# GNN kernel: whole-row unpack, sums, catch-up and epilogue at other places, 64-column pairs, DVE scaling of the last groups

## The reference

```python
# layer 0
deg = jnp.clip(jnp.sum(adj, axis=1, keepdims=True) + 1.0, 1.0, None)
h_neigh = (adj @ X + X) / deg
z = jnp.concatenate([X, h_neigh], axis=1) @ W + b
out = jax.nn.relu(z); norm = jnp.linalg.norm(out, axis=1, keepdims=True)
layer0 = out / jnp.maximum(norm, 1e-12)
x = _layernorm(x + layer0)
# layer 1
deg = jnp.sum(adj, axis=1, keepdims=True)
neigh = adj @ x / (deg + 1.0)
x = _layernorm(x + jnp.concatenate([x, neigh], axis=-1) @ W1.T)
```

## Time and profile before

| | |
|---|---|
| median of 3 runs | 778.35 us (778.16 to 779.37) |
| profiled execution | 778.61 us |
| its span, first to last instruction | 776.7 us |
| granted TensorE clock, mean | 0.96 |
| PE busy | 662.5 us, 85% |
| PEld busy | 610.1 us, 79% |
| DVE busy | 710.8 us, 92% |
| ACT busy | 619.5 us, 80% |
| POOL busy | 211.1 us, 27% |
| read from HBM | 270.6 MB |

### The profile page before, as it was taken

One profiled execution on the slowest core, in us unless ns is written; L12 is line 12 of the kernel. 1 busy time (PEld: TensorE's weight loads), 2 busy tenths in 40 slices (PEclk: granted clock), 3 DMA queues, 4 the chain that ended last, 5 costly groups with the idle time before them and its releaser, 6 DMA issues.

```text
span 776.7 us, 28012 instructions
## 1 busy us (share of the span) xinstructions
PE 662.5 (85%) x11173; PEld 610.1 (79%) x11173; DVE 710.8 (92%) x2703; ACT 619.5 (80%) x848; POOL 211.1 (27%) x302
## 2 busy tenths in 40 slices
PE   1457777878788888989899999999999999999992
PEld 0357677878677787878798989989998989988992
DVE  4699988999999999999999999999999999988894
ACT  4879798999989898989898988887888988840037
POOL 2225433535333332424313030211102020201024
PEclk9978897989999999999999999999999999999997
DMA  9999999999999999999999999999999999800004
GB/s 302 386 420 420 416 410 420 420 419 419 417 420 421 402 420 404 418 416 415 413 402 418 381 420 372 400 360 408 381 398 386 395 383 387 349 2 3 3 21 93
DMA packets 46125, 274.55 MB, mean 353 GB/s; under 512 B 12647, under 2 KB 12711, under 8 KB 13223
## 3 DMA queue, kind: packets, MB, share of 16 engines
q1 hardware_dynamic: 45184, 270.55, 87.0%
q0 software_dynamic: 576, 2.10, 0.8%
q10 hardware_dynamic: 230, 0.07, 0.0%
HBM read 270.60 MB, written 2.10 MB: 351 GB/s over the span
## 4 chain that ended last, share of the span: by engine, by line
DVE 31%; PE 27%; DMA 12%; issue 12%; ACT 10%; POOL 7%; ACTq 0%; DVEq 0%; SPq 0%; POOLq 0%
PE s_ps L367 13%; DMA a_in<-in_adj 9%; DVE e L766 9%; ACT junk L557 7%; DVE t_sb L773 6%; POOL small L1119 6%; PE u_ps L385 4%; PE p_ps L353 3%; DMA xl<-in_x 3%; DVE q_sb L839 2%; DVE y_sb L833 2%; DVE u_sb L773 2%; DVE a_in L773 1%; PE z_ps L431 1%; PE p_ps L442 1%
## 5 line engine op out<-in xcount | busy, mean ns | idle before, releaser
L557 ACT ACTIVATE junk<-a_in 128x2048 uint8<-128x2048 uint16 x256 | 489.6, 1919 | 3.1 <-DMA a_in<-in_adj 3.0
L367 PE MATMUL s_ps<-xh,t_sb 128*128 128x129 f16 x4096 | 377.9, 247 | 22.9 <-DVE t_sb L773 20.2
L367 PEld LDWEIGHTS s_ps<-xh,t_sb 128*128 128x128 fp8e4 x4096 | 306.2, 100 | 50.5 <-DVE t_sb L773 24.7
L766 DVE TENSOR_SCALAR e<-a_in 128x2048 fp8e4<-128x2048 f32 x256 | 310.7, 1224 | 7.8 <-DMA a_in<-in_adj 6.9
L1127 POOL COPY store<-pk 128x32 uint32<-128x32 uint32 (+1 forms) x250 | 130.2, 562 | 312.0 <-ACT pk L566 312.0
L353 PE MATMUL p_ps<-pow_bf,e 128*128 128x16 bf16 x4096 | 141.8, 170 | 62.7 <-DVE e L766 58.9
L353 PEld LDWEIGHTS p_ps<-pow_bf,e 128*128 128x128 fp8e4 x4096 | 128.9, 96 | 79.2 <-DVE e L766 72.9
L773 DVE TENSOR_SCALAR t_sb<-pk 128x128 uint32<-128x128 uint32 x1024 | 150.8, 222 | 5.3 <-ACT pk L566 4.8
L1119 POOL TENSOR_TENSOR small<-small,minus_half 128x4 f32<-128x4 f32 x32 | 74.6, 2332 | 203.9 <-DVE small L827 162.5
L385 PE MATMUL u_ps<-xh,u_sb 128*128 128x128 f16 x1488 | 99.2, 218 | 0.0
L385 PEld LDWEIGHTS u_ps<-xh,u_sb 128*128 128x128 fp8e4 x1488 | 88.9, 97 | 1.2
(11 more groups left out here) (110 smaller groups left out, 486.9 us busy)
## 6 DMA issues: line engine op xcount, KB each, us to landing
a_in<-in_adj SPq DMA_DIRECT2D x256, 1024.0 KB, 10.3
xl<-in_x POOLq DMA_DIRECT2D x4, 512.0 KB, 16.1
out_h<-e SPq DMA_DIRECT2D x8, 256.0 KB, 2.6
b_sb<-in_L_gnn_b ACTq DMA_DIRECT2D x3, 0.2 KB
w_sb<-in_L_gnn_W ACTq DMA_DIRECT2D x1, 32.0 KB
w_raw<-in_L_gnn_W ACTq DMA_DIRECT2D x1, 32.0 KB
```

The costliest lines, as they stand in the source:

```text
L367: last = nc.tensor.matmul(s_ps[:, n % 2, at:GW], t_sb[:, b, :], xh[:, b, at:GW], start=(b == 0), stop=False)
L557: nc.scalar.activation(junk[:, t % 2, :], halves[t % R], ACT.Copy, scale=1.0 / 128, accum_out=half_sum[:, n, c:c + 1]).then_inc(s_half, 1)
L766: nc.vector.tensor_scalar(e8[:, c, :], a_in[:, t % R, :], 1.0, None, ALU.is_equal, saturate=False).then_inc(s_e, 1)
```

## The change

- **Unpack**: a whole row at once (8 operations instead of 16 half as wide), and t_sb has two buffers. s_t and s_sum count whole rows.
- **Order on PE**: in block n the quarters are now 1, 2, 3 of block n-2 and 0 of block n-1; the catch-up of block n-1 is in chunks 0 and 1 of block n. transpose_cat is behind the quarter of (k, c) = (2, 2), dense ahead of pack (2, 3), transpose_h at the end of (3, 3), dense_h behind pack (0, 1) of the next block. Weights are taken after block 0's packs.
- **Order on DVE, ScalarE and POOL**: moved to match. low_part and begin_acc now stand between compare (n,1) and compare (n,2) of a block with k = 0.
- **Pairs**: catch-up and the tail sums of the second half use two accumulated matmuls of 64 columns with the same weights, in place of one of 128; DVE then adds once instead of twice.
- **End**: the last group's squares and their sums are made by DVE, and DVE scales output groups 4 to 7 with one operation each.
- **Buffers**: h_sb, h_t, w1_raw and the small bias tiles now lie in other tiles.

```diff
+NA = 4
-        t_sb = sb("t_sb", [P, NB, P], FP8)
+        t_sb = sb("t_sb", [P, 2, NB, P], FP8)
+        h_t = cat_t[0:F, :, :]
+        w1_raw = agg_flat[0:F, 0:P]
+        def quarter(n, c):
+            return (n - 1, 0) if c == 3 else (n - 2, c + 1)
@@ sync
-                sp.wait_ge(s_o, g + 1)
+                if g < NA:
+                    sp.wait_ge(s_o, g + 1)
+                else:
+                    sp.wait_ge(s_o_dve, g - NA + 1)
@@ tensor
             def sum_quarter(n, i):
-                if i % 2 == 0:
-                    pe.wait_ge(s_t, n * 2 + i // 2 + 1)
+                if i == 0:
+                    pe.wait_ge(s_t, n + 1)
...
             def catch_up(n, half_of):
...
                     for b in range(W):
-                        last = nc.tensor.matmul(u_rows[:, r, :], u_sb[:, r * W + b, :],
-                                                xh[:, low(q - 1) + b, 0:HP], start=(b == 0), stop=(b == W - 1))
+                        for part in range(2):
+                            last = nc.tensor.matmul(u_rows[:, r, 0:F], u_sb[:, r * W + b, :],
+                                                    xh[:, low(q - 1) + b, part * F:(part + 1) * F],
+                                                    start=(b + part == 0), stop=(b + part == W))
...
-            for n in range(NB):
+            for n in range(1, NB):
                 e, k = n // BR - 1, n % BR
-                if e >= 0 and k == 2:
-                    dense(e)
                 for c in range(NC):
+                    if e >= 0 and (k, c) == (2, 3):
+                        dense(e)
                     pack_chunk(n, c)
-                    if e >= 0 and (k, c) == (1, 3):
+                    if e >= 1 and (k, c) == (0, 1):
+                        dense_h(e - 1)
+                    if n > 1 or c == 3:
+                        sum_quarter(*quarter(n, c))
+                    if n > START[1] and c < 2:
+                        catch_up(n - 1, c)
+                    if e >= 0 and (k, c) == (2, 2):
                         transpose_cat(e)
-                    if n == START[seg(n)] and n and c == 0:
-                        pe.wait_ge(s_glo, low(seg(n)) // BR)
-                    if n:
-                        sum_quarter(n - 1, c)
-                    if e >= 0 and (k, c) == (3, 0):
+                    if e >= 0 and (k, c) == (3, 3):
                         transpose_h(e)
-                    if n >= START[1] and c in (1, 2):
-                        catch_up(n, c - 1)
-                    if e >= 0 and (k, c) == (3, 1):
-                        dense_h(e)
             e = NE - 1
+            sum_quarter(NB - 2, 1)
+            dense_h(e - 1)
+            catch_up(NB - 1, 0)
+            sum_quarter(NB - 2, 2)
+            catch_up(NB - 1, 1)
+            sum_quarter(NB - 2, 3)
@@ scalar
                 sum_codes(n, 0)
-                if e >= 0 and k == 2:
-                    take_z(e)
+                if e >= 1 and k == 0:
+                    take_h(e - 1)
+                if n:
+                    take_packed(n - 1, 1)
                 sum_codes(n, 1)
-                if n:
-                    take_packed(n - 1, 1)
-                if n >= 2:
-                    take_sums(n - 2)
-                if e >= 0 and k == 3:
-                    take_h(e)
+                if e >= 1 and k == 0:
+                    take_g(e - 1)
                 sum_codes(n, 2)
                 take_packed(n, 0)
-                if e >= 0 and k == 3:
-                    take_g(e)
+                if e >= 0 and k == 2:
+                    take_cat(e)
                 sum_codes(n, 3)
-                if e >= 0 and k == 1:
-                    take_cat(e)
+                if n >= 2:
+                    take_sums(n - 2)
+                if e >= 0 and k == 2:
+                    take_z(e)
...
-            for g in range(NV + 1):
-                if g < NV:
-                    squares(g)
-                if g:
+            for g in range(NV - 1):
+                squares(g)
+                if 1 <= g <= NA:
                     finish(g - 1)
@@ vector
-            def unpack(n, h):
-                dve.wait_ge(s_pk, n * 2 + h + 1)
-                if n:
-                    dve.wait_ge(s_sum, (n - 1) * 2 + h + 1)
+            def unpack(n):
+                dve.wait_ge(s_pk, n * 2 + 2)
+                if n >= 2:
+                    dve.wait_ge(s_sum, n - 1)
...
-                link(nc.vector.tensor_tensor(rows, u_rows[:, 0:r1 - r0, 0:F], rows, ALU.add))
-                nc.vector.tensor_tensor(rows, u_rows[:, 0:r1 - r0, F:HP], rows, ALU.add).then_inc(s_uadd, 1)
+                nc.vector.tensor_tensor(rows, u_rows[:, 0:r1 - r0, 0:F], rows, ALU.add).then_inc(s_uadd, 1)
...
+            def last_variance():
+                rows = slice(NB - TG, NB)
+                dve.wait_ge(s_vadd, 2 * NV)
+                dve.wait_ge(s_fvar, NV - 4)
+                for n in range(NB - TG, NB):
+                    ins = nc.vector.scalar_tensor_tensor(out=sqf[:, (NV - 1) % 4, n % TG, :], in0=acc[:, n, :], scalar=1.0,
+                                                         in1=acc[:, n, :], op0=ALU.mult, op1=ALU.mult,
+                                                         accum_out=fvar[:, 1, n:n + 1])
+                link(ins)
+                nc.vector.scalar_tensor_tensor(out=fvar[:, 1, rows], in0=fvar[:, 1, rows], scalar=1.0 / F,
+                                               in1=fvar[:, 0, rows], op0=ALU.mult, op1=ALU.add).then_inc(s_fvar, 1)
+            def scale_rows(g):
+                rows = slice(g * TG, (g + 1) * TG)
+                dve.wait_ge(s_froot, g + 1)
+                dve.wait_ge(s_out[g % 4], 16)
+                nc.vector.tensor_tensor(o_sb[:, g % 4, :, :], acc[:, rows, :], bc(fvar[:, 1, rows], TG),
+                                        ALU.mult).then_inc(s_o_dve, 1)
...
                 compare(n, 0)
-                if n:
-                    unpack(n - 1, 0)
                 if e >= 0 and k == 3:
-                    normalise(e)
-                if n > START[1]:
-                    add_piece(n - 1)
+                    norm(e)
                 compare(n, 1)
-                if n >= START[1]:
-                    unpack_piece(n)
                 if e >= 0 and k == 2:
-                    norm(e)
+                    mean(e)
+                if e >= 1 and k == 0:
+                    low_part(e - 1)
+                    begin_acc(e - 1)
                 compare(n, 2)
                 if n:
-                    unpack(n - 1, 1)
-                if e >= 0 and k == 1:
-                    mean(e)
+                    unpack(n - 1)
+                if e >= 0 and k == 3:
+                    residual(e)
                 compare(n, 3)
+                if n > START[1]:
+                    add_piece(n - 1)
+                if n >= START[1]:
+                    unpack_piece(n)
+                if e >= 0 and k == 3:
+                    normalise(e)
...
-                if e >= 0 and k == 2:
-                    residual(e)
-                if e >= 0 and k == 3:
-                    low_part(e)
-                    begin_acc(e)
...
             for g in range(NV):
+                if g >= 4:
+                    variance(g - 1)
+                if g >= NA + 2:
+                    scale_rows(g - 2)
                 add_tail(NV + g)
...
-            variance(NV - 1)
+            last_variance()
+            scale_rows(NV - 2)
+            scale_rows(NV - 1)
```

More of the change, by code:

```diff
@@ L161, in gnn_kernel @@
         b0_sb = sb("b0_sb", [3, F], F32)
[L162 to L165, removed]
         b0_rows = sb("b0_rows", [3, BR, F], BF16)
         ones_bf = sb("ones_bf", [3, P], BF16)
+        h_t = cat_t[0:F, :, :]
+        b0_rest, b0_sum, b0_one = (q_sb[0:3, i, :] for i in range(3))
+        b0_part = q_sb[0:3, 3, 0:F // 2].bitcast(BF16)
         x_in = xl[:, :, 0:F]
@@ L364, in sum_quarter @@
                     pe.wait_ge(s_xlo, i + 1)
+                if n + 1 < NB and n + 1 == START[seg(n + 1)] and n and i * CB < lows(n):
+                    pe.wait_ge(s_glo, min(lows(n), (i + 1) * CB) // BR)
                 for b in range(i * CB, (i + 1) * CB):
                     at = 0 if b < lows(n) else HP
-                    last = nc.tensor.matmul(s_ps[:, n % 2, at:GW], t_sb[:, b, :], xh[:, b, at:GW],
+                    last = nc.tensor.matmul(s_ps[:, n % 2, at:GW], t_sb[:, n % 2, b, :], xh[:, b, at:GW],
                                             start=(b == 0), stop=False)
@@ L441, in tail_sums @@
                     for b in range(W):
-                        last = nc.tensor.matmul(v_ps[j % 3][:, r, :], v_sb[:, j % VR, r * W + b, :],
-                                                xh[:, at + b, 0:HP], start=(b == 0), stop=(b == W - 1))
+                        if j < NV:
+                            last = nc.tensor.matmul(v_ps[j % 3][:, r, :], v_sb[:, j % VR, r * W + b, :],
```

(22 more changed lines are left out.)

79 lines of the change are left out of this document (41 added, 38 removed).

## The result

The changed kernel takes 813.61 us (median of 4 runs, 812.86 to 815.08) against 778.62 (4 runs, 778.16 to 779.37): a ratio of 1.0451, 95% interval 1.0433 to 1.0469. Forecast were 796.0 and a range of 775 to 806. The direction was right and the size was not: +35 us in place of +17.8. The profiled execution has a span of 811.1 (before: 776.7).

A forecast was written before the change was run, and what follows sets the result against it. The adj transfer bounds the first half, then PE, full from block 44, with DVE fuller just before. The last sum ends at 722.0, 24.0 later; less 6.2 at the end gives +17.8 on 778.35: 796 us, range 775 to 806.

The forecast's parts named there:

- Whole-row unpack, "can give back 2.9": Blocks 28-35: cheaper DVE unpack and one add fewer bring block 36 forward by 2.9 us, ends 0 and 5.8.
- the lock: At low_part DVE waits for PE's dense_h, PE for compares queued behind; priced at 19.7 us from block 36.
- The new place of low_part, 19.7 us: Behind dense_h, DVE's delayed compares make PE wait three times a group; 19.7 us in seven groups, 0 to 24.
- dense right behind transpose_cat, 0.83 each: PE waits 0.83 us for ScalarE's copy, seven times from block 36 on: 5.8 us.
- the rival in which only the middle wait remains: Behind dense_h PE still has queued work, so 7 x 1.37 us replaces 19.7: 786 us, chance 0.11.
- the 3.0 behind transpose_h: PE's wait of 0.43 us behind transpose_h is kept, seven times from block 36 on: 3.0 us.
- Work moved past the stream, 5.8: Later sums, catch-up and one dense_h add 5.8 us of PE work from block 36 on, with nothing to cover it.
- Pairs, 0 (-3.9 to 3.9): Catch-up and tail: 1544 pairs of 64-column matmuls at 55.9 ns, as one of 128 columns; no change, ends -3.9 and +3.9.
- The end, -6.2: Behind PE's last tail sum 9.2 us remain instead of 15.4: 6.2 us saved, between 5 and 7.5.
- Start, 0: Block 0 no longer waits for weights, but later blocks go at the transfer's rate: 0, at most 2 us either way.
- the pairs are dear: Rival, catch-up and tail: short matmuls not sustained at 28 ns cost 3.1 us per ns; 811 to 880 us, chance 0.05.
- faster, by relief of DVE: Rival, stages with DVE 97% busy: waits behind begin_acc are covered, 771 to 776, given as 773 us; chance 0.18.

The follow-up runs named there:

- low_part moved: Changed kernel with low_part and begin_acc on VectorE behind compare (n,2) and the unpack, not ahead of compare (n,2): 787.75 us, ratio 1.0107.
- the filled gap: Changed kernel with the pack matmuls of chunk (n,2) in each group's first block issued three times, where PE waits: 812.39 us, ratio 1.0441.
- the lock put into the kernel before: Kernel before with only low_part and begin_acc moved on VectorE, from the end of a group's fourth block to ahead of its compare (n,2): 836.56 us, ratio 1.0736.

## Why the prediction was right or wrong

Between the spans are 34.4 us; 17.8 were forecast. The 16.6 that are missing lie in three places: the start of block 36 (7.4), the stretch from there to the end of the sums (5.3), the end (3.8).

- **Whole-row unpack, "can give back 2.9".** Partly right, but not in this kernel. With low_part moved, blocks 28-35 take 80.3 us and block 36 starts 1.8 earlier than before (0.4 if DVE also makes the second add); the unpack was never run by itself. In the change they take 86.9. The step that failed is "the ends are 0 (the waits below eat it there too) and 5.8": the lock was priced from block 36 on alone, and its low end of 0 did not let block 36 start later than before. It started 4.4 later. Ahead of block 36 the transfer bounds, and I took that as a cover. It is none: the compares that the lock delays also free the transfer's buffers (8.7 us of SyncE's waits for 1.1 without the lock), and PE is at 1.2 GHz for 10.2 us there. How the loss divides between the two is open.
- **The new place of low_part, 19.7 us, the term that decides.** The mechanism is shown: the two calls moved take the waits for compares from 18.7 to 4.0 and the time down by 26 us. Its waits were sized slightly too high: 28.5 us of all kinds were forecast from block 36 on, and 23.4 came. Behind dense_h 0.65, 1.37 and 0.49 were forecast; in the group shown 0.43 and 1.21 came, and the third is filled by the quarter that ran at 1.2 GHz; in the two groups before it is 0.3. So the rival in which only the middle wait remains did not come. What was missing is that a gap can cost more than its length. PE was at 1.2 GHz for 10.2 us beside such gaps from block 36 on, which costs up to 5.1, and my sum has only durations at the full clock. In this stretch the two errors, 5.1 too much of waits and 5.1 of clock left out, hide each other by luck.
- **dense right behind transpose_cat, 0.83 each.** 0.67 each, seven times, 4.7 us: the length is nearly right, and that it adds to the time is not shown. Where it was covered and norm was out of the way, nothing was gained. In a chain in which DVE is the late one PE's waits may not be simply added up; the same caution holds for the 3.0 behind transpose_h.
- **Work moved past the stream, 5.8.** In the kernel with low_part moved the stretch from block 36 to the end of the sums is 322.4 us against 309.2. 5.8 for this, 2.9 more waits than before and 3.6 for the pairs make 12.3 of those 13.2. It wasn't tested by itself.
- **Pairs, 0 (-3.9 to 3.9).** A pair takes 59.4 ns in the stream, where I took 55.9 and had 58.4 as the upper end. From block 36 on that is 3.6 us (1032 pairs), in the tail 2.0, together more than the 3.9 of the upper end. Yet the pairs are a gain, because the add that they save counted for more: 3.5 us net of their price. The sum had that add in two places, in DVE's relief of 2.9 us and in the chain at the end.
- **The end, -6.2.** -2.4. The tail sums take 1.6 us more, which the sum had as 0 under the pairs. In place of 9.2 us behind the last matmul there are 11.5: 1.3 for the add that is late, 0.4 for POOL's root (2.02, not 1.65), 0.9 for the output (5.15 from the end of the scaling, not 4.3), less 0.3 for the squares. The step that failed here is the first of these: I read the end as a chain that starts at PE's end, without looking at what stands on DVE's queue ahead of its first link.
- **Start, 0.** Right: block 28 starts at 306.2 where it was 306.0.

The stretch from block 36 to the end of the sums adds up so: 302.0 of PE's work, 5.8 moved, 23.4 waits, 5.1 clock, 3.6 pairs are 339.9 of 341.6; 1.7 stay open. Of the rivals, "the pairs are dear" has a small part in it, 5.6 us on PE; "faster, by relief of DVE" holds for the pairs alone (775.53). What keeps the kernel with low_part moved 8.3 us above the one before is, by this sum, the moved work above all; no run took that out. The pairs cost PE 3.6 us there, but taking them out makes it 7.3 us slower.

## What to carry to other kernels

Before an operation that waits for another engine is put ahead on an in-order queue, list what that other engine needs from behind it: a lead of several chunks that the two engines had is spent in one such place, and busy times alone don't show it, for both engines get emptier. Price it as a loop, with all that hangs on the late engine (here also the buffers of a transfer that seemed to bound), and not as a sum of one engine's gaps. Such a place is cheap to test: move the call behind the next product that the other engine waits for, which here was worth 26 us in the stream and, with the pairs in both, about 1 us in the tail.

## What the runs showed of the hardware

- Short matmuls back to back: a pair of 64-column f16 matmuls takes 59.4 to 59.7 ns, 29.7 to 29.9 each, against 55.9 for one of 128 columns. For the gap of isolated matmuls the Trainium skill (TensorE: Matmul & The Clock Gate, Back-to-back issue gap) gives columns/2.4 + 2.5 ns, 29.2 each; this stream, with a weight load for each matmul, is within 3% of it.
- TensorE's clock fell to 1.2 GHz in a kernel whose PE is busy 89 to 93% of a stage: behind a wait of 1.21 us at 683.90, a quarter of a sum ran at half speed for 3.29 us. In the kernel before, with waits up to 0.8 us after 389 and one of 1.73 at 377, the clock stayed at 2.4 GHz. In the kernel after there are, from 306 to the end of the sums, fourteen waits above 0.9 us and five stretches at 1.2 GHz (3.4 us each, one of 6.8), so most such waits have none beside them, and the filled gap left the question open. With the lock put into the kernel before, each of the ten waits of 3.28 us after 306 has such a stretch, which begins at most 1.5 us before and 1.3 us behind the wait's end.
- POOL's root of 128x8 takes 1.64 or 2.02 to 2.18 us in the same tail. It takes 2.02 where DVE scales beside it (803.18 beside 803.02), 2.18 where DVE unpacks, and 1.64 at 792.48, where DVE adds; that DVE's kind of work is the cause wasn't tested.
